# Graph network, last quads of the first edge pass: roots by logarithm and exponential, the carry ahead of the exponentials, the scaling of quotients moved

## The reference

```
score = exp(clip(sum over each head of (K[src] * Q[dst] / sqrt(12) * E), -5, 5))
h     = segment_sum(V[src] * score, dst) / (segment_sum(score, dst) + 1e-6)
x     = (y - mean(y)) / sqrt(var(y) + 1e-5),   y = x + h
```

## Time and profile before

| what | us |
|---|---|
| median of 3 runs | 4448.03 |
| the runs | 4444.66 to 4450.70 |
| the profiled execution's own time | 4444.6 |
| its span | 4442.8 |
| mean granted TensorE clock, share of full speed | 0.692 |
| busy: PE / DVE / ACT / POOL | 2622.2 / 1994.1 / 1397.3 / 3209.6 |
| first pass, from the first exponential to the start of the second pass's gathers | 55.5 to 1191.9 |

### The profile page before, as it was taken

One profiled execution on the slowest core, in us unless ns is written; L12 is line 12 of the kernel. 1 busy time (PEld: TensorE's weight loads), 2 busy tenths in 40 slices (PEclk: granted clock), 3 DMA queues, 4 the chain that ended last, 5 costly groups with the idle time before them and its releaser, 6 DMA issues.

```text
span 4442.8 us, 56823 instructions
## 1 busy us (share of the span) xinstructions
PE 2622.2 (59%) x15402; PEld 2238.4 (50%) x15402; DVE 1994.1 (45%) x4498; ACT 1397.3 (31%) x4325; POOL 3209.6 (72%) x3366
## 2 busy tenths in 40 slices
PE   6777887887676667666756643343344333344435
PEld 5666666666566666666634433333343333333334
DVE  3766666666576666666661111111124222222225
ACT  1222222224444444444453322222222222222223
POOL 4777777776277777777757777777776777777776
PEclk7999889897588888888875555555555555555556
DMA  6876676766333333333312122211122111121112
GB/s 192 221 189 184 182 185 182 185 185 170 96 102 99 99 99 99 101 100 99 97 40 40 40 40 40 40 40 40 40 44 51 40 40 39 40 40 39 40 40 55
DMA packets 337337, 409.95 MB, mean 92 GB/s; under 512 B 212209, under 2 KB 248676, under 8 KB 336942
## 3 DMA queue, kind: packets, MB, share of 16 engines
q0 software_dynamic: 133120, 245.58, 23.3%
q1 hardware_dynamic: 203917, 160.75, 13.5%
HBM read 386.26 MB, written 19.77 MB: 91 GB/s over the span
## 4 chain that ended last, share of the span: by engine, by line
POOL 32%; issue 27%; PE 23%; DVE 11%; DMA 5%; ACT 1%; SPq 1%; ACTq 0%; DVEq 0%; POOLq 0%
POOL rows L547 31%; PE bank L639 18%; DVE same L1534 5%; DVE same L1234 3%; DMA rows<-kv_table,src_idx 2%; PE bank L840 1%; DMA rows<-pair_table,src_idx 1%; DVE prod L1306 1%; DVE score L1308 1%; POOL acc_max L574 1%; DVE prod L1304 1%; PE bank L684 1%; PE bank L652 0%; PE bank L653 0%; PE bank L744 0%
## 5 line engine op out<-in xcount | busy, mean ns | idle before, releaser
L639 PE MATMUL bank<-same,rows 128*96 128x128 f32 x4992 | 1086.0, 389 | 1123.9 <-issue 1044.0
L639 PEld LDWEIGHTS bank<-same,rows 128*96 128x96 f32 x4992 | 926.3, 248 | 1257.4 <-issue 1251.5
L547 POOL DMA_INDIRECT rows<-kv_table,src_idx x832 | 793.7, 954 | 318.8 <-issue 238.9
L547 POOL DMA_INDIRECT rows<-pair_table,src_idx x832 | 787.0, 946 | 317.5 <-issue 249.2
L927 ACT COPY acc<-bank 96x511 f32 (+1 forms) x832 | 481.0, 578 | 1647.1 <-PE bank L639 1645.8
L547 POOL DMA_INDIRECT rows<-h_table,src_idx x832 | 790.2, 950 | 272.3 <-issue 253.3
L547 POOL DMA_INDIRECT rows<-ci_table,src_idx x832 | 785.0, 944 | 261.6 <-issue 253.3
L1234 DVE TENSOR_TENSOR same<-bank,rank_col 128x512 f32<-128x512 f32 x624 | 422.9, 678 | 842.7 <-PE bank L639 842.7
L1534 DVE TENSOR_SCALAR same<-iota_s,rank_col,src_hi 128x128 f32<-128x128 f32 x832 | 240.4, 351 | 754.5 <-PE bank L639 754.3
L639 PEld LDWEIGHTS bank<-same,msg 128*105 128x105 f32 x1664 | 232.1, 197 | 306.6 <-DVE same L1234 199.2
L652 PE MATMUL bank<-weights,first_only 97*128 97x96 f32 x1664 | 355.5, 299 | 38.6 <-DMA first_only<-q_table 32.8
(11 more groups left out here) (169 smaller groups left out, 3241.4 us busy)
## 6 DMA issues: line engine op xcount, KB each, us to landing
first_only<-in_attr_cols SPq DMA_DIRECT2D x104, 384.0 KB
first_only<-q_table SPq DMA_DIRECT2D x832, 48.0 KB
first_only<-rank_rows SPq DMA_DIRECT2D x104, 256.0 KB
first_only<-keep_rows SPq DMA_DIRECT2D x104, 192.0 KB, 3.1
rows<-kv_table,src_idx POOLq DMA_INDIRECT x832
rows<-pair_table,src_idx POOLq DMA_INDIRECT x832
rows<-ci_table,src_idx POOLq DMA_INDIRECT x832
rows<-h_table,src_idx POOLq DMA_INDIRECT x832
```

The source lines that it names most:

```text
L547: pool.indirect_dma_start(rows[:, k, j, 0:width], None, table, bass.IndirectOffsetOnAxis(ap=src_idx[:, t:t + 1], axis=0)).then_inc(rows_in ...
L639: mm = pe.matmul(out[0:nrow, here], left(j), right(j), start=(j == 0), stop=(j == TQ - 1), skip_group_check=True)
```

## The change

Four edits. A table set that holds logarithm and exponential is loaded at the start of ACT's program. In the first pass the root of a chunk is Exp(0.5 Ln(var + eps)), two instructions with a wait between them, in place of one Sqrt. In slots 197 to 207 the carry of the quad before is queued ahead of the exponentials instead of behind them. `scale1` stands behind the one-hot matrix of its slot, ahead of the wait for the exponentials, instead of ahead of `picks`. The roots of later passes remain Sqrt.

```diff
+        log_done = sem("log_done")
...
         def _(act):
+            act.preload_act_table_set("natural_log_exp_and_others")
...
+            def root_by_log(c):
+                here = dev[:, c % 2, 0:len(tiles_of(c))]
+                wait(act, a_var, c + 1)
+                act.activation(here, moments[:, c % 2, 0:len(tiles_of(c)), 1], ACT.Ln, bias=eps[:, 0:1]).then_inc(log_done, 1)
+                wait(act, log_done, c + 1)
+                act.activation(here, here, ACT.Exp, scale=0.5).then_inc(counts(a_dev), 1)
...
                 for c in ripe(slot, 1):
-                    root(c, a_var, a_dev)
+                    root_by_log(c)
...
                     q = i * GQ + k
+                    if ripe(q, 1):
+                        spread0(q - 1, (k - 1) % GQ)
                     wait(act, clip_done, q + 1)
                     wait(act, s0.agg_done, q - 1)
                     act.activation(weight_of[k % 2], score[:], ACT.Exp)
                     act.activation(msg[:, k % 2, :, F:SC], score[:], ACT.Exp).then_inc(exp_done, 1)
-                    if not (static(q) and q == 0):
+                    if q > 0 and not ripe(q, 1):
                         spread0(q - 1, (k - 1) % GQ)
...
-                    if static(q):
-                        for c in ripe(q, 2):
-                            scale1(c)
                     if not (static(q) and q == NQ - 1):
                         picks(q + 1, i if k < GQ - 1 else i + 1, (k + 1) % GQ)
...
                     one_hot(same[:, k % 2], iota_over, rank_col, q, P).then_inc(s0.same_done.sem, 1)
+                    for c in ripe(q, 2):
+                        scale1(c)
                     wait(dve, exp_done, q + 1)
```

## The result

The changed kernel takes 4438.9 us (median of 20 runs, 4430.0 to 4445.9) against 4448.6 (median of 20, 4443.7 to 4453.1): a ratio of 0.9979, 95% interval 0.9973 to 0.9985, 9.7 us or 0.2%. The prediction was 4445.0 in 4438 to 4450. The range holds the time, 0.9 us above its lower end, but the gain is well over the 3 us that were forecast: 9.7 us, or 2.7 times the 3.6 us that lie between the 4448.6 of these runs and the forecast 4445.0. Its runs spread over 16 us, those of before over 9.

What follows compares the result with a forecast made beforehand. POOL's gathers hold most of the chain; slots before the second pass move the end one for one. Terms −1.4 − 0.8 + 0.3 + 0.3 = −1.6 us, or −4.2 with full-clock stretches; middle −3: 4448.0 − 3.0 = 4445.0, range 4438 to 4450.

Steps and rivals of the forecast that it cites:

- the clock rival: First-pass slots: PE (TensorE) stays at full clock, 7.8 us a slot, over 20 us saved, 4425; chance 0.12.
- the 0.2% that I had given 0.12: Whole kernel: chance 0.12 of being faster by over 0.2% (8.9 us), mostly from PE staying at full clock.
- my own signs of being wrong: Slots: carries 9.6 us or less apart at half clock, 10.1 or more, or the clock of the slots rising.
- What bounds: Between first and second pass: POOL's gathers hold most of the chain; slot savings or costs move the end one for one.
- Loads at nothing: ACT in the first pass: 21 table loads, 26.9 us busy, go; hardly any on the chain, so worth nothing in themselves.
- carry at −0.44: End of a slot: the carry's copy no longer waits for two exponentials, 0.56 becomes 0.12, −0.44 us a slot.
- The root pair at +0.30: ACT's root: Ln must end before Exp starts, +0.30 us on the loop through moments and root; bounds +0.2 to +0.6.
- Scaling moved: DVE's `scale1` moved: worth nothing in slots 201 to 207, but counts in slot 198; 0.6 us a slot if cover is gone.
- First slots: Slots 197 to 200: carry gains most; next copy after 197 −3.2 us, carry 199 −1.9, −1.4 left at slot 201.
- The clock: TensorE in the slots: half clock throughout gives −1.6 us; the same full-clock stretches as before, −4.2; middle taken, −3.
- its version at half strength: First-pass slots: PE at full clock in half of the slots, giving 4436.
- Degrees: Second pass's start: new 1.28 us load ahead of the Sqrt against 1.3 us of slack; nothing, from above 0.3 us.

Runs made afterwards that it cites:

- changed again: The changed kernel run once more without further edits, against the kernel before: ratio 0.9987 (0.9973 to 1.0002); nine slots 83.8 us at clock 0.62.
- the changed kernel's third: Third profile of the changed kernel, no further edits; one run, no ratio: tail 119.9 us, nine slots 79.4 us at clock 0.74.

## Why the prediction was right or wrong, step by step

- *The number.* The median lies in the range, by 0.9 us, and that is partly luck: the range reached down to 4438 for the clock rival and for the movement of a median, not for the sum. The ratio of 0.9979 is just past the 0.2% that I had given 0.12, and one of my own signs of being wrong came: the clock of the slots rose.
- *What bounds.* Right. The tail moved, and the second pass began 17.5 us earlier in the profile; that pass's last gather was 16.9 us earlier, and the third pass began 17.1 earlier.
- *Loads at nothing, carry at −0.44.* At half clock the sum was right, the split wrong. I read the row of the exponentials at 1141.74 as a wait for the aggregation that ended at 1141.62. It was the load's end at 1141.73; the code has them wait for an older aggregation. With the loads gone and the carry where it was, the slot takes the same 9.89. Where the clock is high, neither edit pays alone and the two together take the copy from 1.4 us behind the aggregation to 0.12.
- *The root pair at +0.30.* Right in kind, a little less in size: +0.24 from start to copy, and 0.25 us a slot when one instruction of it is taken away.
- *Scaling moved.* Nothing in slots 201 to 207, as forecast. In slot 198, where I had it matter, the scaling moved alone gained nothing that shows (10.0 us at clock 0.50).
- *First slots.* The copy came 0.12 behind aggregation 196, as forecast; slot 197 took 7.0 us (6.9 forecast). Slot 198 took 8.4 instead of 10.4, since TensorE was partly at full clock in it (0.69).
- *The clock.* This is the step that failed: the sum had −2.6 us at most for the clock, and the runs put about 6 us on it (next point). I took half clock nearly throughout, or at best the few stretches of before (−1.6 to −4.2 us in all), and so −3 us. All three profiles of the changed kernel show more: 0.77, 0.62 and 0.74 in the nine slots, against 0.53 and 0.51. Measured slots of 9.90 and 7.85 at the two levels agree with my 9.93 and 7.8; so the rival that I gave 0.12 had the mechanism and the price of a slot, and its version at half strength, for which I had 4436, comes within 3 us of the measured 4438.9. I kept it small because a stretch of 70 us at 0.50 with TensorE busy for 58 of it looked like proof that dense work stays slow. It was proof only for that slot's pattern, with 1.34 us of gap every 10.07 us. With the gap filled in the kernel before, the clock was 0.78. The Trainium skill, "TensorE: Matmul & The Clock Gate", Part 1, has activity release the throttle; by that rule the filled kernel should come up, and the trace agrees over the nine slots (0.78 against 0.53), though not in every slot.
- *How much is clock, how much path.* At nearly the same clock (0.78 and 0.77) the nine slots take 83.7 us with the old order, filled, and 77.0 with the new. From the old order's 89.5 at 0.53, about 6 us come with the clock and 7 with the new order, that is, with the loads gone and the carry ahead together. The second part grows with the clock: at 0.64 and 0.62 (scaling moved alone; changed again) the two orders take 85.7 and 83.8, and at half clock they differ by 0.17 us a slot. These are single profiles, and at 0.74 to 0.78 those with the new order vary between 77.0 and 79.4, so the split is good to some 2 us.
- *Degrees.* I set 1.3 us of slack against 1.28, and 0.3 us from above. POOL's seventeenth gather waited 0.89 us, 0.59 more than its usual 0.30:

```profile
1194.92 0.95 POOL L548 DMA_INDIRECT rows<-pair_table,src_idx  x1 [0.89 <-PE bank L640]
```

  The term was too small by 0.3 us. Of the eight profiles with that load ahead of the copy, seven have this gather waiting for 0.88 to 3.02 us (all but the changed kernel's third); in the six without it, or with the root behind the copy, it waits no longer than usual. That the load does it by delaying SP's spread of the degrees is argued, not shown.

The tails of five profiles put the gain at 11 us: the mean of 130.0 and 132.9 less that of 114.2, 127.2 and 119.9. Their nine slots, which late rows do not touch, put it at 9.6. Both agree with the medians' 9.7.

Why the new order has the clock high in more slots stays open. The gap is one candidate: filled, it goes with clocks of 0.78 in the old order and 0.88, 0.87 and 0.78 in the new, against 0.51 to 0.64 and 0.62 to 0.77 unfilled. But the shorter gap of a half-clock slot is not enough, as the logarithm alone has the same 0.93 us and a clock of 0.59. After an aggregation at full clock the old order and the logarithm alone leave TensorE idle for 2.2 us (above), the changed kernel for 0.92:

```profile
1112.35 0.58 PE L672 MATMUL bank<-ident,acc 105*128 105x105 f32 x4 [0.92 <-ACT acc L933]
```

That may be what lets a fast slot follow a fast slot; no run tested it. Which slots are fast differs from run to run, and no run fixed it.

## What to carry to other kernels

A slot's time at the present clock is only half of its price. Where TensorE sits at 1.2 GHz with short regular gaps, work out the slot at both levels and ask what would hold it at the faster one; here what stood ahead of the carry cost 0.44 us at half clock and 1.3 us behind an aggregation at full clock, and there it was the table load and, once that was gone, the scores. Where an instruction starts right behind a table load, look first whether it waited for the load and not for a semaphore that fired shortly before. Moving the carry ahead of the load without removing the load brought the load into the open.

## What the runs showed of the hardware that was not expected

- TensorE's granted clock over nine slots was 0.78 instead of 0.53 when three matmuls of no use (1.3 us a slot at half clock, an estimate from the 0.86 us that two of them add to TensorE's busy time) stood in its gaps, and the slots were 6 us shorter in spite of the added work. Two slots filled in this way stayed at 0.50 all the same.
- The same program showed clocks of 0.77, 0.62 and 0.74 in the same nine slots, and times for them of 77.0, 83.8 and 79.4 us; the kernel before had 0.53 and 0.51, 89.5 and 89.8. So in these profiles the changed kernel varies more from run to run.
- Some chips land gathered rows more slowly: 1231 to 1250 us instead of 1039 for one pass's gathers, the whole kernel 17% longer, with the half-clock slots of the tail unchanged to 0.01 us (10.07, and 9.89 or 9.90).
